# A macaron block on one core: new orders for the iterations in which only the second feed-forward stream is left

## The reference

```
x = x + 0.5 * ffn(layernorm(x))      # first stream, "f1"
x = x + attention(layernorm(x))      # "at"
x = x + 0.5 * ffn(layernorm(x))      # second stream, "f2"
```

## Time and profile before

| | us |
|---|---|
| median of 3 executions (774.02 to 774.63) | 774.03 |
| the profiled execution | 772.65 |
| its span | 770.8 |
| TensorE busy | 724.6 (94%) |
| VectorE busy | 584.3 (76%) |
| ScalarE busy | 602.0 (78%) |
| GpSimd busy | 685.4 (89%) |
| granted clock over the span | 0.997 |

### The profile page before, as it was taken

One profiled execution on the slowest core, in us unless ns is written; L12 is line 12 of the kernel. 1 busy time (PEld: TensorE's weight loads), 2 busy tenths in 40 slices (PEclk: granted clock), 3 DMA queues, 4 the chain that ended last, 5 costly groups with the idle time before them and its releaser, 6 DMA issues.

```text
span 770.8 us, 13299 instructions
## 1 busy us (share of the span) xinstructions
PE 724.6 (94%) x3736; PEld 592.4 (77%) x3736; DVE 584.3 (76%) x1834; ACT 602.0 (78%) x1221; POOL 685.4 (89%) x663
## 2 busy tenths in 40 slices
PE   6899888789999999999999999999999999899888
PEld 6677676668888878888888888888887877777666
DVE  4767887887778797978778797978778587785554
ACT  4688767587888889788888889788878776767876
POOL 3899887879999999999999999999999877686986
PEclk9999999999999999999999999999999999999999
DMA  5553303212233332213333331323333302123331
GB/s 185 192 194 111 111 3 109 95 44 87 107 111 124 111 125 107 77 63 101 123 111 124 111 125 48 114 76 110 124 111 124 112 14 111 36 90 124 122 110 43
DMA packets 31176, 79.38 MB, mean 103 GB/s; under 512 B 3328, under 2 KB 14464, under 8 KB 31104
## 3 DMA queue, kind: packets, MB, share of 16 engines
q1 hardware_dynamic: 30816, 78.47, 29.9%
q10 hardware_dynamic: 288, 0.07, 0.1%
HBM read 73.81 MB, written 4.72 MB: 102 GB/s over the span
## 4 chain that ended last, share of the span: by engine, by line
PE 29%; DVE 27%; POOL 16%; issue 13%; ACT 11%; DMA 3%; DVEq 1%; POOLq 0%; ACTq 0%; SPq 0%
POOL h_lo L942 9%; DVE hid L1129 7%; PE bank L532 4%; PE bank L534 3%; PE bank L533 3%; PE bank L555 3%; POOL root_f L934 3%; PE bank L557 3%; PE bank L556 3%; ACT h_hi L792 3%; ACT hid L781 3%; DVE pick_f L1107 2%; DMA g_all_f<-rows_f 2%; PE bank L651 2%; PE bank L639 2%
## 5 line engine op out<-in xcount | busy, mean ns | idle before, releaser
L942 POOL TENSOR_TENSOR h_lo<-hid,h_hi 128x512 fp32r<-128x512 f32 x383 | 492.1, 1310 | 47.1 <-ACT h_hi L792 46.3
L1129 DVE SCALAR_TENSOR_TENSOR hid<-bank,g_all_f 128x512 f32<-128x512 f32 x384 | 262.6, 684 | 126.0 <-PE bank L534 87.9
L781 ACT ACTIVATE hid<-hid 128x512 f32<-128x512 f32 x384 | 229.6, 621 | 26.7 <-DVE hid L1129 26.1
L792 ACT ACTIVATE h_hi<-hid 128x512 fp32r<-128x512 f32 x384 | 229.0, 622 | 9.0 <-ACT hid L781 0.8
L532 PE MATMUL bank<-x_hi_f,w_hi 128*128 128x512 f32 x384 | 163.9, 427 | 13.5 <-DVE hid L1129 13.4
L555 PE MATMUL bank<-h_hi,w_hi 128*128 128x512 f32 x384 | 153.5, 400 | 4.7 <-POOL h_lo L942 4.5
L557 PE MATMUL bank<-h_hi,w_lo 128*128 128x512 f32 x384 | 152.1, 396 | 0.0
L534 PE MATMUL bank<-x_hi_f,w_lo 128*128 128x512 f32 x384 | 151.6, 395 | 0.0
L533 PE MATMUL bank<-x_lo_f,w_hi 128*128 128x512 f32 x384 | 151.5, 395 | 0.0
L556 PE MATMUL bank<-h_lo,w_hi 128*128 128x512 f32 x384 | 151.3, 394 | 0.0
L532 PEld LDWEIGHTS bank<-x_hi_f,w_hi 128*128 128x128 f32 x384 | 72.8, 190 | 37.4 <-DVE hid L1129 20.7
(11 more groups left out here) (118 smaller groups left out, 1050.4 us busy)
## 6 DMA issues: line engine op xcount, KB each, us to landing
g_all_f<-rows_f SPq DMA_DIRECT2D x128, 512.0 KB, 5.5
x_sb<-in_x SPq DMA_DIRECT2D x16, 256.0 KB, 3.4
out_x<-x_sb SPq DMA_DIRECT2D x15, 256.0 KB, 7.0
g_all_f<-in_w SPq DMA_DIRECT2D x2, 768.0 KB, 6.8
con<-in_const SPq DMA_DIRECT2D x1, 584.0 KB, 6.3
rows_f<-g_row_f SPq DMA_DIRECT2D x32, 16.0 KB, 1.4
out_x<-x_sb SPq DMA_DIRECT2D x2, 128.0 KB, 1.8
g_all_f<-in_wqkv SPq DMA_DIRECT2D x1, 192.0 KB, 6.5
```

The costliest lines, as they stand in the source:

```text
L781: fn(h, h, ACT.Square).then_inc(s_sq[s], 1)
L792: fn(h_hi[:, c, :], hid[:, c % STAGE, :], ACT.Copy).then_inc(s_hhi[s], 1)
L942: gp.tensor_tensor(h_lo[:, c, :], hid[:, c % STAGE, :], h_hi[:, c, :].bitcast(F32), ALU.subtract).then_inc(s_hlo[s], 1)
L1129: v.scalar_tensor_tensor(hid[:, c % STAGE, :], hp[c % 2][:], 0.0, g_all[s][:, EXPERT[c], :], ALU.max, ALU.mult).then_inc(s_z[s], 1)
```

## The change

The iterations t = 15 to 21 (`t >= NG - 1`) get a function of their own, `lone_iteration`, on TensorE, ScalarE, GpSimd and VectorE. All others keep `iteration`. SP sends the gates of group t - 3 at the end of iteration t, where it sent those of group t - 4 at the start; in t = 15 it sends both. The arithmetic and the instructions are the same, but for the filler transpositions, which stay in t = 15 and go in t = 16 and 17.

```diff
 # SP
             def iteration(t, par):
-                broadcast("f2", t + 1 - SHIFT)
+                if not alone("f2", t - 2):
+                    broadcast("f2", t + 1 - SHIFT)
                 broadcast("f1", t + 2)
...
                 if not alone("f2", t - 1):
                     store(t - SHIFT)
+                else:
+                    broadcast("f2", t + 2 - SHIFT)
 # TensorE, state()
-                if alone("f2", n + 1):
+                if alone("f2", n + 1) and not alone("f2", n):
                     keep_busy(a1, 16)
 # TensorE
+            def lone_iteration(t, par):
+                quarter(t, 0, par)
+                state(t - 2)
+                if not alone("f2", t - 2):
+                    weight_rows("f2", t + 1 - SHIFT, t, 1)
+                transpose("at", t - 1, t, 2)
+                quarter(t, 1, par)
+                attend(t - 2)
+                transpose("f2", t + 2 - SHIFT, t, 3)
+                quarter(t, 2, par)
+                logits("f2", t + 2 - SHIFT)
+                quarter(t, 3, par)
+                attn_transpose(t - 2)
+                q(t - 1)
+                quarter(t, 4, par)
+                out_proj(t - 2)
+                quarter(t, 5, par)
+                kv(t - 1, 0)
+                kv(t - 1, 1)
+                quarter(t, 6, par)
+                weight_rows("f2", t + 2 - SHIFT, t, 4)
+                quarter(t, 7, par)
+                if final("f2", t - SHIFT):
+                    last_back()
+                else:
+                    back("f2", t - SHIFT)
 # ScalarE
+            def lone_iteration(t, par):
+                squares(t - 1, 7)
+                norm("at", t - 1)
+                squares(t, 0)
+                if not alone("f2", t - 2):
+                    rows_of_weights("f2", t + 1 - SHIFT)
+                evacuate_x("at", t - 1, t, 1)
+                norm("f2", t + 2 - SHIFT)
+                squares(t, 1)
+                evacuate_x("f2", t + 2 - SHIFT, t, 2)
+                squares(t, 2)
+                exp_logits("f2", t + 2 - SHIFT)
+                squares(t, 3)
+                copy_attnT(t - 2)
+                squares(t, 4)
+                exp_q(t - 1)
+                squares(t, 5)
+                squares(t, 6)
+                copy_v(t - 1)
+                rows_of_weights("f2", t + 2 - SHIFT)
+                copy_yT("f2", t - SHIFT, t)
+                exp_k(t - 1)
 # GpSimd
+            def lone_iteration(t, par):
+                remainders(t - 1, 21, 22, 23)
+                remainders(t, 0, 1, 2, 3, 4)
+                low_part("at", t - 1, 0)
+                remainders(t, 5, 6, 7, 8, 9, 10)
+                low_part("f2", t + 2 - SHIFT, (par + SHIFT) % 2)
+                remainders(t, 11, 12)
+                root_of_weights("f2", t + 2 - SHIFT)
+                remainders(t, 13, 14, 15)
+                inv_std("at", t)
+                remainders(t, 16, 17, 18, 19, 20)
+                inv_std("f2", t + 3 - SHIFT)
+            pipeline(pool, lambda t, par: (lone_iteration if t >= NG - 1 else iteration)(t, par))
 # VectorE
+            def lone_iteration(t, par):
+                n2 = t + 2 - SHIFT
+                if final("f2", t - 1 - SHIFT):
+                    last_remainder()
+                    last_add()
+                if not alone("f2", t - 2):
+                    k_features(t - 2)
+                    q_features(t - 2)
+                weighted(t, 0)
+                if not alone("f2", t - 2):
+                    spread_roots("f2", n2 - 1, 0)
+                    spread_roots("f2", n2 - 1, 1)
+                elif not final("f2", t - 1 - SHIFT):
+                    add_moe("f2", t - 1 - SHIFT)
+                weighted(t, 2)
+                add_moe("f1", t)
+                mask_state(t - 2)
+                weighted(t, 4)
+                high_part("at", t - 1, 0)
+                weighted(t, 6)
+                normalise(t - 2, 0)
+                normalise(t - 2, 1)
+                weighted(t, 8)
+                normalise(t - 2, 2)
+                weighted(t, 10)
+                high_part("f2", n2, (par + SHIFT) % 2)
+                take_sigmoid("f2", n2)
+                best_two("f2", n2)
+                where_two("f2", n2)
+                weighted(t, 12)
+                rope_q_sin(t - 1)
+                weigh_two("f2", n2, 0)
+                weigh_two("f2", n2, 1)
+                weighted(t, 14)
+                rope_q_cos(t - 1)
+                choose_two("f2", n2)
+                rope_q_sum(t - 1)
+                weighted(t, 16)
+                add_attention(t - 2)
+                stats("at", t, 0)
+                mean_variance("at", t)
+                weighted(t, 18)
+                spread_roots("f2", n2, 0)
+                rope_k(t - 1, 0)
+                spread_roots("f2", n2, 1)
+                rope_k(t - 1, 1)
+                weighted(t, 20)
+                rope_k_sum(t - 1)
+                stats("f2", t + 3 - SHIFT, 0)
+                mean_variance("f2", t + 3 - SHIFT)
+                weighted(t, 22)
+                q_features(t - 1)
+                k_features(t - 1)
+            pipeline(dve, lambda t, par: (lone_iteration if t >= NG - 1 else iteration)(t, par))
```

More of the change, by code:

```diff
@@ L693, in iteration @@
                     back("f1", t)
-                if not alone("f2", t - 1):
-                    back("f2", t - SHIFT)
+                back("f2", t - SHIFT)
                 transpose("f2", t + 2 - SHIFT, t, 3)
@@ L706, in iteration @@
                 quarter(t, 7, par)
-                if final("f2", t - SHIFT):
-                    last_back()
-                elif alone("f2", t - 1):
-                    back("f2", t - SHIFT)
                 if not alone("f1", t):
                     back("f1", t + 1)
-            pipeline(pe, iteration)
+            pipeline(pe, lambda t, par: (lone_iteration if t >= NG - 1 else iteration)(t, par))
         @block.scalar
@@ L856, in iteration @@
                     evacuate_x("at", t - 1, t, 1)
-                if not alone("f2", t - 1):
-                    copy_yT("f2", n2_last, t)
+                copy_yT("f2", n2_last, t)
                 squares(t, 2)
@@ L876, in iteration @@
                     copy_yT("f1", n1, t)
-                if alone("f2", t - 1):
-                    copy_yT("f2", n2_last, t)
                 squares(t, 6)
@@ L884, in _ @@
             minus_one = c_mone
-            pipeline(act, iteration)
+            pipeline(act, lambda t, par: (lone_iteration if t >= NG - 1 else iteration)(t, par))
         @block.gpsimd
@@ L975, in iteration @@
                     inv_std_ahead()
-            pipeline(pool, iteration)
+            def lone_iteration(t, par):
[11 more added lines that the diff above has]
+            pipeline(pool, lambda t, par: (lone_iteration if t >= NG - 1 else iteration)(t, par))
         @block.vector
@@ L1252, in iteration @@
                     split_attention_weights()
-                if final("f2", t - 1 - SHIFT):
-                    last_remainder()
-                    last_add()
-                elif alone("f2", t - 2):
-                    add_moe("f2", t - 1 - SHIFT)
                 k_features(t - 2)
@@ L1301, in iteration @@
                     add_moe("f1", t)
-                if not alone("f2", t - 1):
-                    add_moe("f2", t - SHIFT)
+                add_moe("f2", t - SHIFT)
                 weighted(t, 15)
@@ L1329, in iteration @@
                 rope_k_sum(t - 1)
-            pipeline(dve, iteration)
+            def lone_iteration(t, par):
[52 more added lines that the diff above has]
+            pipeline(dve, lambda t, par: (lone_iteration if t >= NG - 1 else iteration)(t, par))
 _INS = ["x", "wqkv", "wout", "router", "w1", "w2", "const"]
```

## The result

The changed kernel takes 783.52 us (median of 4 executions, 782.12 to 785.31) against 774.02 us: a ratio of 1.0124, 95% interval 1.0107 to 1.0142. That is 9.5 us slower, where 2.5 were forecast, and above the range.

The account below looks back on a forecast made before the run. TensorE's stops were taken as the bound. Changes of +5.9, +1.8, -3.3, -0.3 and -1.6 us in t = 15 to 19 gave +2.5: 774.03 + 2.5 = 776.5 us, 8-in-10 range 767.5 to 780.0.

Parts of the forecast that it names:

- What bounds the kernel: t = 15 to 19: no engine fills its time; TensorE's stops come to 5.2, 5.2, 4.3, 2.7 and 2.4 us.
- the ceiling of 16.5 us: t = 15 to 19: the most that could go, 19.8 us of TensorE stops less 3.3 kept in t = 15.
- What goes: Stops removed: 3.3 and 3.2 us ahead of `state`, 0.7 three times at `attend`, DMA waits 0.8 + 1.8, remainder 1.3, small VectorE stops.
- The rows' wait of 2.4 us in t = 15: TensorE waits 2.4 us between two transpositions sharing a bank, until ScalarE copies the gates' rows; bounds 0 to 2.9.
- The router's place: Logits' input ready 12.1 us after iteration start, TensorE there at 9.2: loses 2.9 us in t = 16, 1.3 in t = 15.
- VectorE's late segment, 1.6 + 0.7 + 1.8: Late in t = 15 and 16, TensorE loses 1.6 us at `kv`, 0.7 at the gates' transposition, 1.8 at `back`.
- the bound: Late stops of t = 15 and 16: together 0 to 6 us, the upper with small gate operations taking 1.0 to 1.1.
- t = 17 and 18: Forecast 23.2 and 21.3 us: `back` waits 0.75 in each, the router's transposition 1.5 in t = 18.
- The clock: Earlier profile's granted clock of 1.00 from 626.7 to 754.9 stood against a fall; stops without filler could lower it.
- rival C: Clock falls to 1.2 GHz for some 3 us, twice, costing 1.5 us each: 779.5 us; chance 0.05.

Follow-up runs that it names:

- the best order: Changed kernel with four lines moved, the gates' transposition late and the router's normalisation early from t = 17 on: 767.29 us, ratio 0.9912 to the kernel before.
- the execution at full clock: Changed kernel plus 16 filler transpositions at two stops, in t = 15 and t = 16: 782.73 us, ratio 1.0114; t = 15 takes 38.0 us.
- the one-line cure: Changed kernel with GpSimd's low part of the attention input ahead of the remainder of place 4: 777.98 us, ratio 1.0070 to the kernel before.
- four moved lines together: Changed kernel with low part, t = 15 rows' copy, attention's addition and output's copy each moved earlier: 769.10 us, ratio 0.9923 to the kernel before.

## Why the prediction was right and wrong, step by step

Where stops are added up here, each is taken with the queue's gap, some 0.15 us more than its bracket shows.

**What bounds the kernel; the ceiling of 16.5 us.** Right that stops of TensorE are what counts. In t = 19 the forecast is met to 0.1 us, and its work of 17.8 us showed in the best orders as 17.6 and 17.7. The ceiling itself was not tested: the best order gained 7.4 us.

**What goes.** Right for the large terms: no stop ahead of `state` and `attend` in t = 16 and 17, none for the remainder in t = 18, no DMA wait for the gates from t = 17 on. The small stops behind VectorE did not all go: 0.4 us stands at two up products of t = 18 and at one of t = 19.

**The rows' wait of 2.4 us in t = 15.** Its size was right (2.41, with the queue's gap 2.6), and so was the remark that it lets ScalarE catch up. It is no stop that can be had back by itself: with the rows first only 1.3 us went (39.6 to 38.3, part of it clock), as the same chain came back at the logits.

**The router's place, 12.1 us to the logits.** Right to 0.1 in t = 16 (losses 0.9 + 2.05, forecast 2.9; the seven terms of TensorE's way add up to 9.3 and not to 9.2, which changes nothing). In t = 15 it is 0.5 in place of 1.3, where the slow products had given ScalarE time, and 1.6 in the execution at full clock. In t = 16 it is the dearest of the new stops, and the one-line cure brought the most of the single moves.

**VectorE's late segment, 1.6 + 0.7 + 1.8.** `kv` 2.3 and 1.7, gates 1.6 and 0.6, `back` 1.6 and 1.6: 5.5 in t = 15 and 3.9 in t = 16 against 4.1 each. Of the missing 1.4 in t = 15, 0.7 stands at `kv` and 0.9 at the gates, where the spread roots took 1.24 us at 661.70; the bound named such times, the value did not.

**t = 17 and 18.** This step failed: "without rotations `back` still waits 0.75 each time", and for the gates the sums leave at most 0.2 and 0.1, with no working. Measured: gates 1.6 and 1.7, `back` 0.4 and 0.4, the router's transposition 1.8 for 1.5, and in t = 18 some 0.8 at two up products. Three small operations that lie on the way to the gates took 3.3 us together, where the walk of t = 15 and 16 has 0.3, 0.1 and, with the reduction behind it, 0.5. I had put long times into the bounds of t = 15 and 16 alone; they fall due wherever GpSimd is in a remainder, and GpSimd is busy 19.1 and 19.6 of 24.0 us there. The two iterations are 0.8 + 2.7 = 3.5 us over the forecast. 1.0 of it in each went with GpSimd's long operations: t = 17 then takes 23.0, where 23.2 were forecast. t = 18 still takes 23.0 against 21.3; what is left there are the two up products' 0.8, which the sum did not have, and `back`, at 1.2 in place of 0.75.

**The clock.** This step failed as well, and by its chance: rival C had 0.05, at 1.5 us twice. Against the earlier trace rows the slow products cost in t = 15 0.4 + 0.65 + 0.58 + 0.58 + 0.5 = 2.7 us (transpositions, three products, `attend`), in t = 16 0.2 + 0.65 + 0.58 + 0.3 = 1.7. What is left of that in the time is less: 1.6 us in t = 15 (39.6 against 38.0 at full clock), and at most 1.7 in t = 16, for which no profile at full clock exists. So the price was about right, and it came on top of the other errors. I held the 1.00 of the earlier trace rows against it; but that row was measured with filler in each long stop, and said nothing on a kernel without. The rule of the Trainium skill, TensorE: Matmul & The Clock Gate, "What's actually happening", that idleness halves the clock, agrees with the 0.50 behind the stops of 3.3 (half of it filler) and 2.4 us and with the run without filler; the stop of 2.41 us behind which the clock stayed at 1.00 shows that not every such stop does it. A row should not be held against a rival when it was measured with the very thing that the change takes out.

The profiled execution missed the forecast by 10.2 us: 1.7 ahead of t = 15, 3.8 in t = 15, 1.3 in t = 16, 0.8 and 2.7 in t = 17 and 18. Of the 3.8, 1.6 is clock, 1.4 the late segment, 0.3 the router's place at full clock, 0.2 the rows, and 0.3 has no place. The 1.3 of t = 16 is the clock's 1.7 less 0.2 of the late segment and rounding. The median missed by 7.0. What stays open: when a stop brings a spell, since the same order had one in t = 15 in two executions of three; how the clock's cost and the stops add in t = 16; and why the filler there was followed by a spell later on.

## What to carry to other kernels

Walk an in-order schedule through all its queues and not by counting what a move takes away: here a three-us stop was removed, and the new order lost nearly as much (2.9 us in t = 16) at the shared buffer alone, whose last reader stood one place too late in GpSimd's queue. A stop taken away alone mostly came back at the next one; four moved lines together, each on one chain, turned +1.2% into -0.8%. Where a kernel has filler, first measure it without, before a change takes it out.

## What the runs showed of the hardware

- A small VectorE operation with two inputs in on-chip memory (SBUF) that started while GpSimd ran a 1.3 us elementwise operation ended only with that one: 1.01 to 1.28 us in t = 17 and 18 of the changed kernel in place of 0.21. GpSimd's power of 1.64 us does not hold it: the choice took 0.21 us at 714.67, with the power running from 714.50 to 716.14.
- The cast of the attention input took 1.42 us before, while GpSimd was busy, and 0.42 in the changed kernel at 642.01, while it was idle.
- Behind a stop of 3.06 us the clock fell, behind one of 2.95 in the next iteration of the same execution it did not. Two executions have the spells in the same iterations, and the same 39.6 and 33.1 us; a third with the same order has only that of t = 16, and takes 38.0 us for t = 15.
